# Pivot rows by transfers in the attention, and a router gate with stationary weights, in a fused transformer kernel

## The chip, the cores and the metric

The kernel runs on one core of a Trainium2 chip. The metric is the device time of one execution, in microseconds (us). TensorE multiplies matrices, VectorE, ScalarE and GpSimd work on tiles, and SyncE issues transfers. The profile calls them PE (PEld for the weight loads), DVE, ACT, POOL and SP.

## The reference, cut to what matters

Eight sequences (B) of 512 tokens (S) with 256 features (E) pass through four blocks: an attention with 16 heads, a mixture of 8 experts, a low-rank spectral product and a quaternion product. The change touches the expert gate and the orthogonalised mode matrix. Everything is float32.

```python
# gate of the experts
xn = rms_w * (x * jax.lax.rsqrt(var + EPS))
gate = xn @ wg_W + wg_b + (genre_embed @ gg_W + gg_b)
gate_w = jax.nn.softmax(gate, axis=-1)
topk_w, topk_i = jax.lax.top_k(gate_w, TOP_K)
...
# mode matrix, 64 x 64
gram = raw.T @ raw
chol = cholesky(gram + 0.0001 * eye, lower=True)
inv_chol = solve_triangular(chol, eye, lower=True)
q = raw @ inv_chol.T
signs = jnp.sign(jnp.sum(q * raw, axis=0, keepdims=True))
```

## The kernel before

**One order for all engines.** Pure Python functions write a list of steps, `order`. Each engine runs through this list in a program of its own and does its part of each step, so the place of a step in the list is its place in every queue. Semaphores carry the dependences. SyncE's program issues the transfers of a step when it comes to it, and waits first for what makes the data.

**Attention** (`attention_order`). There are 32 groups `i`, four to a sequence, of four heads each. A group is cut into 16 places, (k, n) with k and n from 0 to 3, and a place holds one `row` and one `col` step. A `row` step is a product of scores on TensorE (L1155, three PSUM banks in turn) and the maximum of each row on VectorE (L1628), which frees the bank: the product waits for the maximum three before it. A `col` step is the transposed product (L1170, with the mask's product L1174 or a seed by ScalarE L1360) and the exponential on ScalarE (L1355), over two banks. Every second k, a `weigh` pair multiplies the exponentials by the values (L1189): four heads on four groups of 32 columns of TensorE, 17 columns used. The maxima are split in two bf16 parts (`split_maxima`, L1638, L1640), turned on TensorE (`maxima_rows`) and sent by SyncE into the operands of the `col` steps (L967). Between them lie the projections of the next sequence (`project`), whose three bf16 parts are made by ScalarE, VectorE (`rest`) and GpSimd (`part`) and stored by SyncE (L925). At the end of every second k there is a piece of the experts' weights: SyncE stores chunk n-2 (L983), GpSimd splits chunk n-1 (L1864, L1866), SyncE fetches chunk n (L978).

**The chain of a sequence** (`chain`). After its attention each sequence passes its residual, its gate and its routing, one small step to a place. The residual's rows are turned (`turn_x1`, L1216) and copied to `x1T` by ScalarE (L1386), then come four `square_x1` on ScalarE, `root_x1` on GpSimd, four places later the `gate`, one place later `logits`. The gate takes the turned tokens as weights and moves the eight columns of `wg`: 4 tiles of tokens by 2 halves of the features, each float32 product being two instructions (L1227), and one product for the conditioning (L1229). Chains 0 to 5 lie in the attention, 6 and 7 in the experts.

**Experts** (`expert_order`). 39 tiles of 256 routed rows pass three layers (L1084) after their rows are turned (L1247). In a tile four places take a piece of `matrices`, once the chains are over.

**The mode matrix** (`matrices`). `gram` is one product on TensorE; `elim` holds the Gram matrix beside the transposed modes, 64 x 128. Each of the 63 `eliminate` steps spreads pivot row j over the partitions by a TensorE product with a broadcast column of the identity (L1099, two instructions), and VectorE (recorded under the helper's line L845) takes the reciprocal of the pivot, the factors, and the row update. TensorE waits for VectorE's step j-1, VectorE for TensorE's step j. Then come the norms, the quaternions and the combined matrices. Small products on TensorE take banks 6 and 7 in turn (`misc_bank`), and each waits till the one two before it is evicted.

## Time and profile before

| what | us |
|---|---|
| median of three runs | 1160.48 |
| lowest and highest | 1159.94, 1166.9 |
| the profiled execution | 1163.8 |
| its span, first to last instruction | 1162.1 |

The profile is one execution. Its granted TensorE clock is 0.996 of full speed. Busy times are those of an engine's own instructions. The ends of matmuls are modelled, so that neighbours overlap in the record; the distance of their starts is the safer measure. The attention's last row products start at 584 us; the first expert products start at 614 us; the mode matrix's steps lie from 785 to 988 us.

### The profile page before, as it was taken

What the parts mean: (1) busy time and instruction counts of PE and PEld (TensorE: products, weight loads), DVE (VectorE), ACT (ScalarE), POOL (GpSimd) and SP (SyncE); (2) the same over time, 40 slices, a digit from 0 to 9 for tenths busy, and PEclk for the clock granted to TensorE, in tenths of its full rate; (3) what the DMA queues carried; (4) which work ended last, traced back from release to release, by engine and by line L of the source; (5) the groups of instructions that cost most, each with busy time, mean ns of one, the idle gap of its engine ahead of it and who ended that gap; (6) DMA issues with size and microseconds to landing.
All of it is one profiled execution on the core that took longest, in us unless ns stands there. A gap on an engine that the chain in (4) does not pass through costs nothing.

```text
span 1162.1 us, 23399 instructions
## 1 busy us (share of the span) xinstructions
PE 1122.4 (97%) x7520; PEld 763.4 (66%) x7520; DVE 770.8 (66%) x2265; ACT 803.1 (69%) x1752; POOL 512.6 (44%) x837
## 2 busy tenths in 40 slices
PE   8899999999999999998989999999999999999988
PEld 4333434434334343342418999998999999999968
DVE  4877777787887878878745434355555555667747
ACT  2578888787787877877786756655666666666645
POOL 8424135583755837657462365354222223222220
PEclk8999999999999999999999999999999999999999
DMA  8665638367384572843837488856566766723536
GB/s 220 193 195 189 219 100 250 124 215 231 119 257 138 198 235 94 242 157 133 286 101 269 115 309 306 267 120 133 155 193 190 213 193 179 226 48 70 164 91 217
DMA packets 101616, 213.64 MB, mean 184 GB/s; under 512 B 10917, under 2 KB 71341, under 8 KB 93046
## 3 DMA queue, kind: packets, MB, share of 16 engines
q1 hardware_dynamic: 86038, 192.42, 51.1%
q0 software_dynamic: 14304, 18.69, 9.0%
q10 hardware_dynamic: 1152, 1.05, 0.4%
q8 instruction: 59, 0.97, 0.3%
q14 instruction: 63, 0.52, 0.1%
HBM read 239.28 MB, written 74.29 MB: 270 GB/s over the span
## 4 chain that ended last, share of the span: by engine, by line
PE 46%; ACT 3%; issue 1%; DVE 1%; POOL 1%; DMA 1%; another core or an unknown queue 0%; ACTq 0%; POOLq 0%
PE bank L1084 38%; PE bank L1247 1%; PE bank L1189 1%; PE bank L1099 1%; ACT pt L1355 1%; PE bank L1170 1%; DMA x<-yout,rows 1%; PE bank L1113 1%; PE bank L1174 1%; PE bank L1207 1%; PE bank L1282 0%; PE bank L1155 0%; PE bank L1227 0%; ACT full L1433 0%
## 5 line engine op out<-in xcount | busy, mean ns | idle before, releaser
L1628 DVE CUSTOM_DVE_ANT_0 junk<-bank,mneg 128x512 bf16<-128x512 f32 x512 | 333.0, 683 | 119.0 <-PE bank L1155 116.3
L1355 ACT ACTIVATE pt<-bank 128x512 f32<-128x512 f32 x512 | 301.0, 594 | 67.8 <-PE bank L1170 29.7
L1975 POOL DMA_INDIRECT x<-yout,rows x78 | 122.8, 1574 | 292.9 <-ACT yout L1438 249.6
L1084 PE MATMUL bank<-hid,w 128*128 128x256 f32 x1872 | 242.7, 286 | 4.2 <-DVE hid L1776 3.8
L1084 PEld LDWEIGHTS bank<-hid,w 128*128 128x128 f32 x1872 | 229.3, 190 | 6.0 <-issue 4.8
L1776 DVE TENSOR_TENSOR hid<-full,hid 128x256 fp32r<-128x256 f32 x312 | 133.3, 431 | 135.3 <-ACT full L1433 126.8
L1428 ACT ACTIVATE hid<-bank,biases 128x256 fp32r<-128x256 f32 x312 | 149.4, 479 | 91.6 <-PE bank L1084 88.0
L1433 ACT ACTIVATE full<-bank,biases 128x256 f32<-128x256 f32 x312 | 148.7, 477 | 0.0
L1174 PE MATMUL bank<-mneg,identb 128*128 128x512 bf16 x386 | 146.9, 381 | 0.0
L1084 PE MATMUL bank<-rowsT,w 128*128 128x256 f32 x936 | 122.9, 284 | 0.9 <-issue 0.9
L1084 PE MATMUL bank<-w,hid 128*128 128x256 f32 x936 | 121.9, 283 | 1.5 <-DVE hid L1776 1.5
L1189 PE MATMUL bank<-pt,vaug 128*17 128x512 f32 x1024 | 123.1, 598 | 0.0
L1084 PEld LDWEIGHTS bank<-rowsT,w 128*128 128x128 f32 x936 | 116.0, 190 | 1.7 <-issue 1.6
L1084 PEld LDWEIGHTS bank<-w,hid 128*128 128x128 f32 x936 | 115.1, 190 | 1.7 <-issue 1.7
L1438 ACT ACTIVATE yout<-yout,rows 128x256 f32<-128x256 f32 x78 | 39.3, 508 | 96.5 <-DVE yout L1782 96.5
L1170 PE MATMUL bank<-qst,kst 98*128 98x512 bf16 x256 | 97.5, 383 | 8.1 <-ACT pt L1355 6.3
L1155 PE MATMUL bank<-stacks 96*128 96x512 bf16 x256 | 97.6, 386 | 5.6 <-DVE rowmax L1628 4.4
L1155 PE MATMUL bank<-kst,qst 96*128 96x512 bf16 x256 | 97.8, 382 | 5.4 <-DVE rowmax L1628 4.8
L1170 PE MATMUL bank<-stacks 98*128 98x512 bf16 x256 | 97.5, 381 | 1.7 <-ACT pt L1355 1.0
L1866 POOL TENSOR_TENSOR w_parts<-w_parts 128x512 fp32r<-128x512 f32 x64 | 82.2, 1285 | 5.2
L1360 ACT ACTIVATE bank<-mneg 128x512 f32<-128x512 bf16 x124 | 74.6, 602 | 4.0
L1965 POOL DMA_INDIRECT routed<-xw,idx x64 | 64.1, 1001 | 17.1 <-issue 13.5
(184 smaller groups left out, 1445.2 us busy)
## 6 DMA issues: line engine op xcount, KB each, us to landing
w<-split_weights SPq DMA_DIRECT2D x80, 1024.0 KB
w<-split_weights SPq DMA_DIRECT2D x40, 2048.0 KB
split_weights<-w_parts SPq DMA_DIRECT2D x64, 512.0 KB, 3.8
w_parts<-in_W SPq DMA_DIRECT2D x64, 256.0 KB, 4.3
split_parts<-parts SPq DMA_DIRECT2D x28, 384.0 KB, 2.6
rows<-routed SPq DMA_DIRECT2D x39, 258.0 KB, 3.4
stacks<-split_parts SPq DMA_DIRECT2D x36, 256.0 KB, 5.2
qst<-split_parts SPq DMA_DIRECT2D x24, 256.0 KB, 5.3
```

The lines of the kernel that those rows point to most:

```text
L1084: product = T.matmul(ps, w[p], x[q], start=(k == 0 and n == 0), stop=(k == len(weights) - 1 and n == 2))
L1155: T.matmul(bank[n % 3][:, :], qst[b % 2][0:KQ, h, st * P:(st + 1) * P], kst[b % 2][0:KQ, h, :], start=True, stop=True).then_inc(row_scored ...
L1170: product = T.matmul(ps[:, :], kst[b % 2][0:KQ + SHIFTS, h, kt * P:(kt + 1) * P], qst[b % 2][0:KQ + SHIFTS, h, :], start=not seed, stop=li ...
L1174: product = T.matmul(ps[:, :], identb[:, :], mneg[:, 1, kt, :], start=False, stop=True)
L1189: product = T.matmul(bank[5][32 * hh:32 * hh + D + 1, :], vaug[b % 2][:, kt, h, :], pt[col_place[gi, kt, hh] % len(pt)][:, :], start=(kt = ...
L1355: A.activation(pt[n % len(pt)][:, :], bank[3 + n % 2][:, :], ACT.Exp, scale=float(D) ** -0.5).then_inc(exped.sem, 1)
L1428: A.activation((hid1, hid2)[n - 1][j % 2][0][:, m, :], ps[:, 0:TW], ACT.Relu, bias=biases[j % NS][:, column:column + 1])
L1433: A.activation(full[place % len(full)][:, :], ps[:, 0:TW], ACT.Relu, bias=biases[j % NS][:, column:column + 1]).then_inc(rectified.sem, 1)
L1628: V.tensor_tensor_reduce(junk[n % 2][:, :], bank[n % 3][:, :], mneg[:, 0, st, :], 1.0, FLOOR, ALU.add, ALU.max, rowmax[gi % 2][:, hh, st:s ...
L1776: V.tensor_tensor(lo, h[:, :], hi.bitcast(F32), ALU.subtract).then_inc(hidden_low.sem, 1)
L1866: G.tensor_tensor(w_parts[n][:, 1], w_parts[n][:, 1].bitcast(F32), w_parts[n][:, 0].bitcast(F32), ALU.subtract).then_inc(w_low.sem, 1)
L1975: G.indirect_dma_start(x2_dram, bass.IndirectOffsetOnAxis(ap=rows[j % NS][:, tt, E + 1:E + 2].bitcast(U32), axis=0), yout[j % NY][:, tt], ...
```

## The change

- The gate's weights (`wg`, widened with zeros to 32 columns) become the stationary operand, on four column groups, one for each tile of 128 tokens; the tokens (`x1T`) move, 128 columns each. The result has the experts on partitions. ScalarE copies it into `x1T`'s first 128 columns (`gate_rows`), TensorE turns it with one transpose (`turn_gate`), and ScalarE copies the logits (`copy_logits`). `gate`, `gate_rows` and `turn_gate` now lie behind the second, third and fourth `square_x1`, `copy_logits` one place after `root_x1`, and `logits` stays at its place.
- The conditioning's part of the logits is computed once for all sequences (`cond_gate`), from a product `condX` made in `prepare`.
- The pivot row is no longer spread by TensorE. SyncE sends row j of `elim` to 64 partitions of `pivot_row[j % 2]` (`send_pivot`), and VectorE reads it from there. `gram` moves into group 2 of the attention, and 58 eliminations into groups 3 to 31, two a group, at place n = 2 of k = 0 and k = 2, each with the sending of the next pivot at n = 3. Five stay in the experts, with three pieces' pause ahead of each.
- `m2` is stored without gaps, with fewer zeros to set.

```diff
     for st in range(ST):
         out.append(("square_x1", b, st))
         yield
+        if st:
+            out.append((("gate", b), ("gate_rows", b), ("turn_gate", b))[st - 1])
     out.append(("root_x1", b))
+    yield
+    out.append(("copy_logits", b))
     for _ in range(4):
         yield
-    out.append(("gate", b))
-    yield
     out.append(("logits", b))
...
 def matrices(out):
 
-    out.append(("gram",))
-    yield
-    for j in range(KB - 1):
+    for j in range(ATTENTION_PIVOTS, KB - 1):
+        for _ in range(3):
+            yield
         out.append(("eliminate", j))
-        yield
+        if j + 1 < KB - 1:
+            out.append(("send_pivot", j + 1))
...
+                if n == 2 and k % 2 == 0 and PIVOT_GROUP <= i < GROUPS:
+                    j = 2 * (i - PIVOT_GROUP) + k // 2
+                    if j < ATTENTION_PIVOTS:
+                        out.append(("eliminate", j))
+                        pivots.append(("send_pivot", j + 1))
+                if (n, k) == (3, 2) and i == PIVOT_GROUP - 1:
+                    out.append(("gram",))
+                    pivots.append(("send_pivot", 0))
+                elif n == 3 and pivots:
+                    out.append(pivots.pop(0))
...
+            elif name == "send_pivot":
+                j, = at
+                sp.wait_ge(*matrix.at(("eliminate", j - 1) if j else ("gram",)))
+                start(pivot_row[j % 2][:, :], elim[j:j + 1, :].unsqueeze(1).to_broadcast([1, KB, 2 * KB])).then_inc(dma_pivot[j % 2], 16)
...
-            elif name == "eliminate":
-                j, = at
-                ps = take(misc_bank(step))
-                pe.wait_ge(ident_made, 2)
-                pe.wait_ge(*matrix.at(("eliminate", j - 1) if j else ("gram",)))
-                pe.wait_ge(constants_made, CONSTANTS)
-                T.matmul(ps[:, 0:2 * KB], ident[:, j:j + 1].to_broadcast([P, P]), elim[:, :],
-                         start=True, stop=True).then_inc(side_pe.sem, 1)
...
-                for st in range(ST):
-                    for k in range(KT):
-                        T.matmul(ps[:, st * NX:(st + 1) * NX], x1T[:, k, st * P:(st + 1) * P], wg[:, k],
-                                 start=(k == 0), stop=(k == KT - 1))
-                T.matmul(ps[:, ST * NX:(ST + 1) * NX], condR[:, b:b + 1].to_broadcast([C + 2, P]), ggw[:, :],
-                         start=True, stop=True).then_inc(gated.sem, 1)
+                for k in range(KT):
+                    for st in range(ST):
+                        product = T.matmul(ps[GW * st:GW * (st + 1), 0:P], wg[:, k], x1T[:, k, st * P:(st + 1) * P],
+                                           start=(k == 0), stop=(k == KT - 1))
+                product.then_inc(gated.sem, 1)
+            elif name == "turn_gate":
+                b, = at
+                ps = take(misc_bank(step))
+                pe.wait_ge(*gate_rows.at((b,)))
+                pe.wait_ge(ident_made, 2)
+                T.transpose(ps[:, 0:P], x1T[:, 0, 0:P], ident[:, :]).then_inc(gate_turned.sem, 1)
...
-                ps, _ = misc_bank(step)
+                row = pivot_row[j % 2]
                 dve.wait_ge(constants_made, CONSTANTS)
-                dve.wait_ge(*side_pe.at(step))
-                v(V.reciprocal, pivot[:, 0:1], ps[0:KB, j:j + 1])
+                dve.wait_ge(dma_pivot[j % 2], 16 * (j // 2 + 1))
+                v(V.reciprocal, pivot[:, 0:1], row[:, j:j + 1])
                 v(V.scalar_tensor_tensor, pivot[:, 1:2], elim[0:KB, j:j + 1], pivot[:, 0:1], below[:, j:j + 1], ALU.mult, ALU.mult)
-                v(V.scalar_tensor_tensor, elim[0:KB, :], ps[0:KB, 0:2 * KB], pivot[:, 1:2], elim[0:KB, :], ALU.mult, ALU.add)
+                v(V.scalar_tensor_tensor, elim[:, :], row[:, :], pivot[:, 1:2], elim[:, :], ALU.mult, ALU.add)
```

## Rows read from the trace of the kernel before

**Rows 1.** Busy time by stretch: PE, PEld, DVE, ACT, POOL, clock, DMA, GB/s.

```profile
250.00:300.00 50.00, 49.92 (x288) 22.60 (x281) 38.57 (x116) 39.31 (x81) 26.09 (x65) 1.00 0.68 205
...
1000.00:1050.00 50.00, 50.00 (x422) 50.00 (x421) 32.76 (x106) 32.38 (x80) 12.44 (x8) 1.00 0.40 83
```

**Rows 2.** TensorE groups by form: count, busy us, mean ns, idle us before.

```profile
L1099 PE MATMUL bank<-elim,ident 128*128 128x128 f32 x126 | 24.2, 273 | 2.4 <-DVE elim L845 1.4 <-issue 0.9
```

**Rows 3.** Timeline of TensorE, experts: start us, us, line, operation, count.

```profile
856.42 0.60 PE L1247 MATMUL bank<-ident,rows 128*128 128x128 f32 x4
...
869.17 0.60 PE L1247 MATMUL bank<-ident,rows 128*128 128x128 f32 x4
...
1008.16 0.60 PE L1247 MATMUL bank<-ident,rows 128*128 128x128 f32 x4
...
1020.05 0.60 PE L1247 MATMUL bank<-ident,rows 128*128 128x128 f32 x4
```

**Rows 4.** Timeline of TensorE at the fourth elimination step; idle time in brackets.

```profile
797.40 0.46 PE L1099 MATMUL bank<-elim,ident 128*128 128x128 f32 x2 [1.44 <-DVE elim L845]
```

**Rows 5.** Timeline of TensorE at a weighing and a gate in the attention.

```profile
200.50 1.91 PE L1189 MATMUL bank<-pt,vaug 128*17 128x512 f32 x16
...
202.34 0.39 PE L1155 MATMUL bank<-stacks 96*128 96x512 bf16 x1
...
202.79 1.85 PE L1227 MATMUL bank<-wg,x1T 128*128 128x8 f32 x16
...
204.72 1.11 PE L1207 MATMUL bank<-wo,oT_last 128*128 128x256 f32 x4
```

**Rows 6.** Timeline of ScalarE and TensorE where the gate's transposition would stand.

```profile
271.32 0.42 ACT L1303 ACTIVATE squared<-xw 128x256 bf16<-128x256 f32 x1
...
271.92 0.38 PE L1155 MATMUL bank<-kst,qst 96*128 96x512 bf16 x1
```

**Rows 7.** VectorE's groups by form, and below them two rows of its timeline.

```profile
L845 DVE RECIPROCAL pivot<-bank 64x1 f32<-64x1 f32 x63 | 9.6, 152 | 0.0
...
L845 DVE SCALAR_TENSOR_TENSOR pivot<-elim,pivot,below 64x1 f32<-64x1 f32 x63 | 13.3, 211 | 2.2
...
L845 DVE SCALAR_TENSOR_TENSOR elim<-bank,pivot,elim 64x128 f32<-64x128 f32 x63 | 21.6, 343 | 2.2
...
L1640 DVE TENSOR_TENSOR m<-rowmax,m 128x16 bf16<-128x16 f32 x32 | 11.6, 362 | 1.1
...
L1472 DVE TENSOR_TENSOR gt<-flts,gs 128x32 f32<-128x32 f32 x16 | 8.2, 516 | 0.6
...
239.49 1.12 DVE L1638 CAST m<-rowmax 128x16 bf16<-128x16 f32 x1
...
240.64 0.23 DVE L1640 TENSOR_TENSOR m<-rowmax,m 128x16 bf16<-128x16 f32 x1
```

**Rows 8.** Waits between 60 and 590 us: total us, times, longest.

```profile
DVE junk L1628 <- PE bank L1155: 109.4, 97, 2.6
```

**Rows 9.** Timeline of VectorE behind the first and the last place of a step.

```profile
61.67 0.08 DVE L1628 DVE_READ_ACCUMULATOR2_ANT rowmax<- 128x1 f32 x1
...
63.40 0.69 DVE L1628 CUSTOM_DVE_ANT_0 junk<-bank,mneg 128x512 bf16<-128x512 f32 x1 [1.65 <-PE bank L1155]
...
580.37 0.08 DVE L1628 DVE_READ_ACCUMULATOR2_ANT rowmax<- 128x1 f32 x1
```

**Rows 10.** Waits of SyncE, its transfers, its timeline, and a row of VectorE's.

```profile
SPq L925 <- POOL parts L1833: 165.8, 28, 14.6
...
split_parts<-parts SPq DMA_DIRECT2D x28, 384.0 KB, 2.6
...
240.56 0.38 SPq L925 DMA_DIRECT2D split_parts<-parts  x1
...
240.98 0.49 SPq L983 DMA_DIRECT2D split_weights<-w_parts  x1
...
242.58 0.08 DVE L1628 DVE_READ_ACCUMULATOR2_ANT rowmax<- 128x1 f32 x1
```

More of the change, by code:

```diff
@@ L53 @@
 TOPK = 2
+GW = P // ST
 NTILES = B * S * TOPK // TW + NX - 1
@@ L259, in finish_steps @@
         return [("project_o", b, st) for st in range(ST)] + [("chain", b)]
-    chains, todo, rests, parted = [], [], [], []
+    chains, todo, rests, parted, pivots = [], [], [], [], []
     def work_off():
@@ L501, in _build @@
     below = lasting("below", [KB, KB])
-    elim = lasting("elim", [P, 2 * KB])
+    elim = lasting("elim", [KB, 2 * KB])
+    pivot_row = [lasting(f"pivot_row{i}", [KB, 2 * KB]) for i in range(2)]
     raw = lasting("raw", [KB, 2, KB])
@@ L565, in _build @@
     rowmax = [sb(f"rowmax{i}", [P, GH, ST]) for i in range(2)]
-    m2 = [sb(f"m2_{i}", [P, ST, P], BF16) for i in range(2)]
+    m2 = [sb(f"m2_{i}", [P, (ST - 1) * GH * SHIFTS + P], BF16) for i in range(2)]
     mrow = [sb(f"mrow{i}", [GH * SHIFTS, S], BF16) for i in range(2)]
@@ L637, in _build @@
     gated = signal("gated", of("gate"))
+    gate_turned = signal("gate_turned", of("turn_gate"))
+    cond_gated = signal("cond_gated", of("cond_gate"))
     counted = signal("counted", of("place"))
-    side_pe = Signal(sem("side_products"), [s for s in order if s[0] in ("gram", "eliminate", "mixed", "combined")])
+    side_pe = Signal(sem("side_products"), [s for s in order if s[0] in ("gram", "mixed", "combined")])
     rows_turned = signal("rows_turned", of("turn"))
@@ L653, in _build @@
     x1T_ready = signal("x1T_ready", of("turn_x1"))
-    logits_ready = signal("logits_ready", of("gate"))
+    gate_rows = signal("gate_rows", of("gate_rows"))
+    logits_ready = signal("logits_ready", of("copy_logits"))
+    cond_ready = signal("cond_ready", of("cond_gate"))
     gate_exped = signal("gate_exped", of("gate_exp"))
@@ L735, in _build @@
     dma_quat = sem("dma_quat")
+    dma_pivot = [sem(f"dma_pivot{i}") for i in range(2)]
     dma_x2 = [sem(f"dma_x2_{i}") for i in range(NL)]
     dma_out = [sem(f"dma_out{i}") for i in range(2)]
-    CONSTANTS = 23
+    CONSTANTS = -1 + 25
     MASKS = 4
@@ L1198, in tensor_program @@
                 for st in range(ST):
-                    product = T.matmul(ps[:, st * P:(st + 1) * P], m2[gi % 2][:, st], identb[:, :], start=True, stop=True)
+                    product = T.matmul(ps[:, st * P:(st + 1) * P], m2[gi % 2][:, st * GH * SHIFTS:st * GH * SHIFTS + P], identb[:, :], start=True, stop=True)
                 product.then_inc(max_turned.sem, 1)
@@ L1632, in vector_program @@
                 found = rowmax[gi % 2][:, :, :]
-                first_part, second_part = (m2[gi % 2][:, :, k * GH:(k + 1) * GH].rearrange("p s h -> p h s") for k in range(SHIFTS))
+                first_part, second_part = (m2[gi % 2][:, 0:ST * GH * SHIFTS].rearrange("p (s k h) -> p k h s", s=ST, k=SHIFTS)[:, k] for k in range(SHIFTS))
                 dve.wait_ge(constants_made, CONSTANTS)
```

60 lines of the change are left out of this document (42 added, 18 removed).

## The prediction

> **What bounds the kernel now.** I read the busy shares by stretch first. In the attention (a stretch around 275 us) and in the experts (1000 to 1050 us) TensorE is busy 49.9 and 50.0 us of 50; VectorE stands at 38.6 and 32.8 [rows 1]. TensorE is the bound in both stages, so what counts is what its queue is relieved of, and what new makes it stand still. Next I read TensorE's own record of the experts, for the pitch of a tile; then its record of a gate; then VectorE's groups and waits in the attention, and last the queue of SyncE, which has to send the pivot rows.
>
> **Experts: 63 matmul pairs leave TensorE.** A group by form gives 24.2 us busy for 126 instructions [rows 2], but that is not their price, because they overlap their neighbours. The tile's pitch is: with four elimination steps in it, it takes from 856.42 to 869.17, 12.75 us; with none, from 1008.16 to 1020.05, 11.89 us [rows 3]. That is 0.215 us a step, and 63 x 0.215 = 13.5 us. Ahead of one pair TensorE stood 1.44 us for VectorE's earlier step [rows 4]; the product behind it waited for nothing else, so 1.4 us more go. Together -14.9; the bounds are -13.5 (the wait is inherited by the next product) and -25.6 (the busy time). The five steps left there use no TensorE; each has three pieces' time to its pivot, some 9 us, and I cost them at nothing. Without that cover each would hold VectorE, and with it the low halves that TensorE's next layer needs.
>
> **Gate: 8 times.** Now it lasts from 204.72 back to 202.79, 1.93 us, with the conditioning pair inside [rows 5]. After: 16 instructions on four column groups, 128 columns each. The kernel has the same pattern in the weighing, 16 instructions with 512 columns in 200.50 to 202.34, 1.84 us [rows 5]. If time goes with columns, the gate takes 0.46; if it goes with instructions, 1.84. I take 0.8: nearer the first, as the columns are a quarter, and above it, as the weight loads do not shrink. The transposition added costs 0.60 / 4 = 0.15, by the transposes of the experts' rows [rows 3]. So 0.95 against 1.93, 8 x -0.98 = -7.8, and +0.3 once for the conditioning product: -7.5, between -10.3 and +0.8. The transposition waits for ScalarE's copy of the gate's rows. ScalarE would reach that place at 271.32 and need some 0.25 us; TensorE would reach its own at 271.92 [rows 6]. So the wait is mostly hidden; for the one batch where it isn't I add 0.5.
>
> The Trainium skill (TensorEngine Tiling (Array Packing), Tiling Modes) says that tiles work independently and can load and multiply in parallel. That speaks for the 0.46; the weighing at 1.84 us for 16 agrees with it as far as it goes.
>
> **Attention: 58 steps join VectorE.** A step is 0.152 + 0.211 + 0.343 us [rows 7], with gaps 0.75. VectorE idles 109.4 us for rows' products between 60 and 590 us [rows 8], and 58 x 0.75 = 44 fits in the sum; but not at every place. A row product waits for the maximum three before it. I laid a delay at each of the 58 places into VectorE's record (the first after the maximum that ends at 61.75, with 1.65 us idle behind it, the last after the one that ends at 580.45), let it run down in the idle times that follow, and counted what went beyond the start of the product three later [rows 9]. That is work on recorded times, not a measurement. It gives 4.4 us at 0.75 us a step, 8.5 at 1.05, 18 at 1.5, 32 at 1.95, 42 at 2.25: steep, since idle time is used up.
>
> What does a step really cost? First, VectorE's operations that read two operands from SBUF are longer here than their shortest: the second part of the maxima has a mean of 362 ns where a single one took 230, a comparison has 516 in the mean, and the cast that leads the maxima's split once took 1.12 us [rows 7]. The pivot row now comes from SBUF, so two of the three operations are of that kind. I add 0.15 each: 1.05 us a step.
>
> The Trainium skill (SBUF — State Buffer, Who interferes with whom) gives the cause: a VectorE instruction with two SBUF inputs locks against a GpSimd instruction that reads SBUF, and one with a single SBUF input does not. By that rule the old step, whose row came from PSUM, was exempt in its last operation and the new one is not. The trace's 362 and 516 agree.
>
> Second, transfers can be late. A pivot is sent one place after the step that makes it and used eight places later, about 9 us. SyncE sends in order, and it stands 165.8 us in all, up to 14.6, before the parts of the projections [rows 10]. The tightest place, in the middle of a batch: SyncE is done with such a part at 240.94 (the chunk's store follows at 240.98), and VectorE's row maxima reach the next step at 242.66 [rows 10]. A part of 384 KB lands 2.6 us after its issue [rows 10]; a pivot behind it lands at about 243.7. So it is about 1 us late. Holding SyncE's record against VectorE's at all 58 places gives such room of 1.7 us at eight (two each in the batches from group 12 to 25), and 4.3 us or more at the others. Eight steps with 1 us more raise the loss from 8.5 to 15.4; with 0.3 to 9.9. Some of what TensorE stands there ScalarE uses to catch up, and I take 13. The ends are 4.4 (no wait, no lock) and 42.
>
> The Trainium skill (DMA: Bandwidth & Descriptors, Queues, rings and completion order) states that the semaphore write of a transfer lands only after earlier writes of that DMA engine. It speaks against the change: a small pivot can't overtake a large part. No row before shows it alone.
>
> SyncE's own 58 issues, about 0.4 us each, lie in its idle time. SyncE now also waits for VectorE at each place; behind it stand the store and fetch of a weight chunk, which have half a group's time to the next. ScalarE gets eight copies of about 0.25 us and loses nothing that counts. I cost these at nothing; if that cover goes, GpSimd's chunk work is late, and after it the parts.
>
> **Sum.** -14.9 - 7.5 + 0.5 + 13 = -8.9 us against the profiled execution of 1163.8 us (span 1162.1), so 1154.9. That execution lies 3.3 us above the median of 1160.5; against the median it is **1151.6 us**.
>
> **Rivals.**
> - *All covered*: no late pivot and no lock, attention loss 4.4. Then -17.5: 1143.0. For it speaks the idle sum; against it the eight tight places. 0.18.
> - *VectorE becomes the bound* (slower): pivots late not at eight places but at most, since SyncE waits for GpSimd, GpSimd for VectorE, and both now slip. At 2.25 us a step the loss is 42, the sum +20: 1180.6. It decides from about 1.75 us a step (loss 22, no gain), and is over 1% slower from 2.0. Against it: 4.3 us of room or more at 50 places. 0.18.
> - *The lock at full strength*: GpSimd is busy 26.1 of 50 us [rows 1]; if each of the two operations meets it half of the time and waits 0.7 us then, a step costs 1.5, and with late pivots the loss is about 25: +3, so 1163.6 against the median. 0.09. The rule is that of the Trainium skill's page SBUF — State Buffer, told above.
> - *The change relieves less*: gate in 1.84 us, the wait inherited: -13.5 + 0.8 + 0.5 + 13 = +0.8, 1161.3. 0.10.
> - *The forecast*: 0.45, by its own terms 1144 to 1158.
>
> **How the numbers follow.** About 1%, 11.6 us, is what a measurement can tell from no change. 1% faster is below 1148.9: all covered, 0.17, and half of the forecast, 0.22; 0.39. Within 1%: the other half, 0.23, and the two cases around 1162, 0.18; 0.41. Slower, over 1172.1: 0.18 and tails, 0.20. The range that leaves 2 in 10 out goes from 1141 to 1173, the slow end into the VectorE case.
>
> **What would show it.** A tile in the experts at 11.9 us throughout from 800 us on. A gate in about 0.8 us. In the attention, idle time of TensorE for VectorE's maxima up by some 10 us, at groups 13, 17, 21 and 25 above all, and VectorE waiting for the pivot's landing at those eight places alone. Two-operand steps with a mean over 230 ns and single ones over 1 us. I am wrong if VectorE waits for pivots all along, if the attention doesn't lengthen, or if the tile still takes 12.7 us.

## The result, and the profile after

| kernel | median us | lowest to highest | span of the profiled execution |
|---|---|---|---|
| before, beside it (four runs) | 1160.31 | 1159.94 to 1166.9 | 1162.1 |
| changed | 1178.28 | 1176.15 to 1180.99 | 1174.4 |

The ratio is 1.0127, with a 95% interval of 1.0096 to 1.0159: slower by 14.7 us. The quotient of the two medians in the table is 1.0155, or 18.0 us, at the far end of that interval; below, the ratio is used. The forecast of 1151.6 was on the wrong side, and its range ended at 1173.

Two places tell where the time went, in the two profiled executions. The last row maximum of the attention ends at 589.7 us before and at 616.1 after, 26.4 later; the end of the span comes only 12.3 later. So the attention lost 26, and the experts gained 14.

First the parts that went as forecast. Busy times by stretch, as in [rows 1], then the timeline of TensorE at four tiles of the experts, as in [rows 3], and the gate in the timeline of TensorE with the groups of its two operations, as in [rows 5]:

```profile
250.00:300.00 50.00, 44.94 (x254) 18.90 (x257) 40.31 (x128) 37.54 (x83) 24.85 (x57) 0.97 0.76 221
1000.00:1050.00 50.00, 50.00 (x425) 50.00 (x424) 20.84 (x47) 32.99 (x80) 14.81 (x10) 1.00 0.59 178
...
855.68 0.60 PE L1279 MATMUL bank<-ident,rows 128*128 128x128 f32 x4
867.43 0.60 PE L1279 MATMUL bank<-ident,rows 128*128 128x128 f32 x4
...
1011.52 0.60 PE L1279 MATMUL bank<-ident,rows 128*128 128x128 f32 x4
1023.43 0.60 PE L1279 MATMUL bank<-ident,rows 128*128 128x128 f32 x4
...
202.98 0.64 PE L1248 MATMUL bank<-x1T,wg 128*32 128x128 f32 x16
203.56 0.39 PE L1176 MATMUL bank<-stacks 96*128 96x512 bf16 x1
...
205.33 0.30 PE L1256 MATMUL bank<-ident,x1T 128*128 128x128 f32 x1 [0.29 <-ACT x1T L1431]
205.47 1.03 PE L1160 MATMUL bank<-wv,xT 128*128 128x256 f32 x4
...
L1248 PE MATMUL bank<-x1T,wg 128*32 128x128 f32 x128 | 5.2, 279 | 0.7
L1256 PE MATMUL bank<-ident,x1T 128*128 128x128 f32 x8 | 2.4, 303 | 2.0 <-ACT x1T L1431 1.8
```

The tile at 855 us took 12.75 before and takes 11.75 now, and the later one still 11.9. A gate is 0.64 us in the record and its transposition 0.30, but the rows behind them start 0.58 and 0.14 later, and the price before (1.93) was such a distance of starts. What is wrong stands in the first line: in the attention TensorE is busy 44.9 of 50 us where it was 49.9.

Then the elimination's groups on VectorE in the attention (60 to 600 us), and its waits there, as in [rows 7, 8]; the second pair of lines is from 60 to 616 us. The 58th step lies behind 600 us, so the groups have 57:

```profile
L870 DVE SCALAR_TENSOR_TENSOR elim<-pivot_row,pivot,elim 64x128 f32<-64x128 f32 x57 | 26.2, 459 | 2.0
L870 DVE SCALAR_TENSOR_TENSOR pivot<-elim,pivot,below 64x1 f32<-64x1 f32 x57 | 18.9, 332 | 2.0
L870 DVE RECIPROCAL pivot<-pivot_row 64x1 f32<-64x1 f32 x57 | 8.6, 151 | 15.9 <-DMA pivot_row<-elim 15.9
...
DVE junk L1671 <- PE bank L1176: 66.2, 80, 1.5
DVE pivot L870 <- DMA pivot_row<-elim: 15.9, 10, 2.7
```

A step is 0.151 + 0.332 + 0.459 us, with gaps some 1.0, as forecast (1.05). VectorE used up 43 of its 109 us of idle time. And it stood 15.9 us for pivot rows, ten times.

Last, one of the four longest of these waits, in the order in which it builds up: SyncE's queue, VectorE, GpSimd beside it, TensorE.

```profile
247.38 0.38 SPq L950 DMA_DIRECT2D split_parts<-parts  x1
247.81 0.49 SPq L1013 DMA_DIRECT2D pivot_row<-elim  x1
...
249.40 0.08 DVE L1671 DVE_READ_ACCUMULATOR2_ANT rowmax<- 128x1 f32 x1
252.05 0.15 DVE L870 RECIPROCAL pivot<-pivot_row 64x1 f32<-64x1 f32 x1 [2.57 <-DMA pivot_row<-elim]
252.24 0.64 DVE L870 SCALAR_TENSOR_TENSOR pivot<-elim,pivot,below 64x1 f32<-64x1 f32 x1
252.92 1.21 DVE L870 SCALAR_TENSOR_TENSOR elim<-pivot_row,pivot,elim 64x128 f32<-64x128 f32 x1
...
251.72 2.26 POOL L1876 TENSOR_TENSOR parts<-rest,parts 128x512 bf16<-128x512 f32 x2
...
249.75 0.38 PE L1191 MATMUL bank<-stacks 98*128 98x512 bf16 x1
249.97 0.38 PE L1176 MATMUL bank<-kst,qst 96*128 96x512 bf16 x1
...
250.61 0.38 PE L1195 MATMUL bank<-mneg,identb 128*128 128x512 bf16 x1
254.79 0.61 PE L1176 MATMUL bank<-kst,qst 96*128 96x512 bf16 x1 [3.80 <-DVE rowmax L1671]
255.19 0.63 PE L1191 MATMUL bank<-stacks 98*128 98x512 bf16 x1
255.62 0.63 PE L1195 MATMUL bank<-mneg,identb 128*128 128x512 bf16 x1
```

SyncE stands for the part until 247.38 and sends the row behind it. The row lands 4.2 us after its issue. VectorE waits 2.57 us, then both two-operand operations are long (0.64 and 1.21 where the shortest are 0.21 and 0.34) beside two operations of GpSimd that fill 251.72 to 253.98, and TensorE stands 3.80 us. Read the starts of TensorE's rows after that: they come every 0.43 us, where the same products came every 0.22 before the stall. TensorE now runs at 1.2 GHz, the lower of its two levels. The same pattern comes at groups 13, 17, 21 and 25. The stretches that follow, with the granted clock in the last column but two:

```profile
254.80:258.20 3.40, 3.40 (x12) 1.47 (x13) 3.37 (x11) 1.62 (x5) 1.88 (x2) 0.50 0.79 238
333.30:336.70 3.40, 3.18 (x12) 1.48 (x12) 3.37 (x10) 2.72 (x8) 1.45 (x2) 0.50 0.90 257
411.80:415.20 3.40, 3.18 (x12) 1.46 (x12) 3.37 (x10) 3.01 (x10) 1.04 (x2) 0.50 0.77 211
486.90:493.70 6.80, 4.45 (x14) 1.93 (x15) 6.38 (x17) 2.64 (x8) 3.20 (x4) 0.50 0.89 281
```

Added up over the whole span, the stretches at 1.2 GHz are 12 us before and 48 us after.

### The profile page after: what moved, and what is told of

Read it like the earlier page. It is cut to its first block, busy times and chain, and to the rows that moved or that the text cites. A ratio compares the mean times of both kernels' runs of the same rounds, so it can differ in the third digit from the quotient of the medians.

```text
span 1174.4 us, 23150 instructions
## 1 busy us (share of the span) xinstructions
PE 1107.8 (94%) x7335; PEld 742.6 (63%) x7388; DVE 777.4 (66%) x2266; ACT 805.4 (69%) x1761; POOL 511.7 (44%) x838
## 3 DMA queue, kind: packets, MB, share of 16 engines
q10 hardware_dynamic: 1152, 1.05, 0.4%
## 4 chain that ended last, share of the span: by engine, by line
PE 41%; DMA 3%; POOL 2%; ACT 1%; issue 1%; DVE 1%; SPq 1%; POOLq 0%; DVEq 0%; ACTq 0%
PE bank L1113 36%; DMA x<-yout,rows 2%; PE bank L1279 1%; PE bank L1228 1%; PE bank L1134 1%; DMA out<-fin 1%; POOL routed L2010 1%; PE bank L1210 1%; PE bank L1176 0%; DMA routed<-xw,idx 0%; POOL x L2020 0%; PE bank L1191 0%; DMA w_parts<-in_W 0%; POOL gt L870 0%; POOL run L870 0%
## 5 line engine op out<-in xcount | busy, mean ns | idle before, releaser
L1113 PE MATMUL bank<-hid,w 128*128 128x256 f32 x1872 | 237.4, 286 | 7.0 <-DVE hid L1819 7.0
L1469 ACT ACTIVATE hid<-bank,biases 128x256 fp32r<-128x256 f32 x312 | 151.9, 487 | 84.8 <-PE bank L1113 84.5
L1474 ACT ACTIVATE full<-bank,biases 128x256 f32<-128x256 f32 x312 | 151.6, 486 | 0.0
L1195 PE MATMUL bank<-mneg,identb 128*128 128x512 bf16 x333 | 129.6, 389 | 0.0
L1113 PE MATMUL bank<-w,hid 128*128 128x256 f32 x936 | 118.6, 282 | 1.5 <-DVE hid L1819 1.5
L1113 PE MATMUL bank<-rowsT,w 128*128 128x256 f32 x936 | 118.1, 282 | 1.7 <-ACT full L1474 0.9
L1176 PE MATMUL bank<-stacks 96*128 96x512 bf16 x256 | 100.5, 398 | 18.0 <-DVE rowmax L1671 15.3
L1908 POOL CAST w_parts<-w_parts 128x512 fp32r<-128x512 f32 x64 | 39.9, 624 | 113.5 <-DMA w_parts<-in_W 113.5
```

What stands on the lines that cost most here:

```text
L1113: product = T.matmul(ps, w[p], x[q], start=(k == 0 and n == 0), stop=(k == len(weights) - 1 and n == 2))
L1176: T.matmul(bank[n % 3][:, :], qst[b % 2][0:KQ, h, st * P:(st + 1) * P], kst[b % 2][0:KQ, h, :], start=True, stop=True).then_inc(row_scored ...
L1195: product = T.matmul(ps[:, :], identb[:, :], mneg[:, 1, kt, :], start=False, stop=True)
L1469: A.activation((hid1, hid2)[n - 1][j % 2][0][:, m, :], ps[:, 0:TW], ACT.Relu, bias=biases[j % NS][:, column:column + 1])
L1474: A.activation(full[place % len(full)][:, :], ps[:, 0:TW], ACT.Relu, bias=biases[j % NS][:, column:column + 1]).then_inc(rectified.sem, 1)
```

## The experiments

Every ratio is against the kernel before on the same chip, with its 95% interval; "us" behind a ratio is its distance from 1, times 1160.3. The intervals are 2 to 6 us either way, so two runs less than some 5 us apart are not told apart. Times of single places, such as the end of the last maximum, are each from one profiled execution.

### 1. The two halves alone

The kernel before, with the gate's part of the change only (its products, `gate_rows`, `turn_gate`, `copy_logits`, `cond_gate`, the gapless `m2`):

> The kernel before with the gate's part of the change alone: weights stationary, the transposition, the conditioning once for all. The pivots stay TensorE products in the experts. My theory (the gate is not at fault; in the changed kernel its eight products take 0.65 us each and the transpositions 0.3, against 1.93 before) expects -7 to -8 us, so about 1153. The rival that the gate at its new place makes TensorE wait expects 1160 or more, with waits of TensorE at the transposition.

Measured: 0.9913 (0.9891 to 0.9935), -10.1 us. The forecast had -7.0 for it, just outside the interval (-7.5).

The changed kernel with the gate as before, so only the pivot rows move:

> The pivots' part of the change alone, the gate as before. If the gate helps by 7 to 8 us also beside the pivots, this is slower than the whole change: about 1186. If the gate is what hurts, it is below 1178.

Measured: 1.0163 (1.0144 to 1.0181), +18.9 us; eleven waits for rows in the whole execution, up to 2.7 us. The whole loss belongs to the pivot rows. The two halves add up to +8.8, the whole change has +14.7; the rest of 6 us is beyond the intervals only narrowly, and I have no cause for it.

### 2. The row ahead of the part

```diff
                         out.append(("eliminate", j))
-                        pivots.append(("send_pivot", j + 1))
+                        out.append(("send_pivot", j + 1))
```

The row is sent right behind its step and no longer behind the part.

> The whole change, with the sending of the pivot row right behind its elimination in SyncE's queue, ahead of the store of a projection's part, for which SyncE waits. In the changed kernel VectorE waits 2.5 to 2.7 us for the pivot row in groups 13, 17, 21 and 25, TensorE then stands up to 3.8 us, and the granted clock falls to half behind each of these places. Theory A (late rows and the clock behind them) expects these four waits and the four spells of half clock to be gone: 4 x 2.5 us of waits and about 8 us of clock, so about 1162, with the waits of 0.7 to 1.1 us in groups 11, 15, 19, 23 still there. Theory B (VectorE's added work of 58 us alone is too much) expects 1172 or more.

Measured: 0.9983 (0.9963 to 1.0002), -2.0 us: 16.7 us better than the change. The waits at groups 13, 17, 21 and 25 fell from 2.5-2.7 us to 0.2-0.7, and TensorE's four stalls from 3.5-3.8 to under 1 us. No stretch at 1.2 GHz is left there. In the four late batches that is 11 us of stalls, and the rest is what comes with them. The total of the waits for rows fell only to 11.9 us, since others grew (3.65 us at group 3; 1.6, 1.2 and 2.0 at k = 0 of groups 11, 19 and 23). The profiled execution took 1167.3 us, 5.6 above the median of its ten, and its last maximum ends at 609.4; so the traces show less of the gain than the times do.

### 3. The clock by itself

The late rows stay, and TensorE gets twelve products of no use ahead of each stall:

```diff
+                if i in (13, 17, 21, 25) and (k, n) == (1, 1):
+                    out.append(("filler", i))
...
+            elif name == "filler":
+                ps = take(misc_bank(step))
+                pe.wait_ge(masks_made, MASKS)
+                for _ in range(12):
+                    product = T.matmul(ps[:, :], identb[:, :], mneg[:, 1, 0, :], start=True, stop=True)
```

> The whole change, with twelve more products of 128x512 bf16 (2.6 us at full clock, results unused) in TensorE's queue in groups 13, 17, 21 and 25, ahead of the product that stands there for up to 3.8 us. The late rows stay. If the half clock follows from TensorE standing still (theory A), the four spells at these places are gone or fewer, the products themselves are covered by the wait, and the time falls by 4 to 8 us, to about 1172. If the clock falls for another reason, or if the products cost more than they cover, the time is 1178 or more and the spells are at their places.

Measured: 1.0082 (1.0055 to 1.0109), +9.5 us. The timeline of TensorE at the same stall, and two of the stretches quoted above:

```profile
250.47 2.75 PE L1258 MATMUL bank<-mneg,identb 128*128 128x512 bf16 x12
254.38 0.39 PE L1179 MATMUL bank<-kst,qst 96*128 96x512 bf16 x1 [1.16 <-DVE rowmax L1680]
254.61 0.38 PE L1194 MATMUL bank<-stacks 98*128 98x512 bf16 x1
...
254.80:258.20 3.40, 3.07 (x17) 1.17 (x16) 3.37 (x12) 2.96 (x9) 1.74 (x2) 1.00 0.81 248
...
486.90:493.70 6.80, 6.47 (x40) 2.02 (x38) 6.34 (x21) 5.72 (x15) 3.95 (x13) 1.00 0.62 186
```

VectorE's rows are as late as before (2.56, 2.57, 2.96 and 2.65 us), and the product behind the stall starts 4.13 us after the last one ahead of it, where it took 4.18. But the clock stays at 2.4 GHz and the starts 0.22 us apart, at all four places. The ratios differ by 5.2 us, with intervals that overlap. The traces say much the same: TensorE's stall where the maxima of the last groups run out ends at 566.7 us and not at 571.8, though the last maximum ends only 3.5 us earlier (612.6), behind a late row at group 31 (1.7 us) that the change does not have. So with 48 products more the attention is some 4 to 5 us shorter, and I take 5 as the clock's price; it is the least certain of the terms. Over the whole span 20 us less are spent at the lower level, 17 of them in the four stretches quoted above, and that gave back 5 and not 10. In three of the four stretches VectorE is busy 3.3 of 3.4 us or more at either clock, so it sets much of the pace itself.

### 4. VectorE's load, SyncE's stops, the transfers

In four versions VectorE reads constant rows and waits for none, so the mode matrix is not computed. They differ in what SyncE does. First nothing:

```diff
-                sp.wait_ge(*matrix.at(("eliminate", j - 1) if j else ("gram",)))
-                start(pivot_row[j % 2][:, :], elim[j:j + 1, :].unsqueeze(1).to_broadcast([1, KB, 2 * KB])).then_inc(dma_pivot[j % 2], 16)
...
-                dve.wait_ge(dma_pivot[j % 2], 16 * (j // 2 + 1))
```

> The whole change without any pivot transfer: VectorE reads constant rows from SBUF, so the mode matrix isn't computed, while VectorE's three operations a step, their places and operands' forms stay. What is left of the loss in the attention is that of VectorE's work and its lock against GpSimd. Theory A expects no wait for rows at all and fewer spells of half clock: about 1158. Theory B expects 1172 or more, and TensorE's waits for row maxima as in the changed kernel.

Then the stop alone: the same kernel, with only the `sp.wait_ge(*matrix.at(...))` of the first removed line put back.

> Constant pivot rows on VectorE and no transfer, as in the run without transfers (1145.6 us), but SyncE still stops at each of the 63 places until VectorE's elimination step before it is done, as in the run with unused transfers (1156.8 us). The mode matrix isn't computed here. If SyncE's stops alone cost (its chunk loads go out later, GpSimd's splits start later and fall beside VectorE's elimination), the time is 1154 to 1159 us, GpSimd's waits for chunks come to about 110 us and the elimination's operations are about 13 us over their minimum. If the transfers themselves cost (queue, memory), the time is 1143 to 1149 us, with GpSimd's waits near 67 us and 6.5 us over the minimum.

Then the stop and a transfer of a constant row, which VectorE doesn't wait for (SyncE itself waits here for its transfer two before, by then some 15 us old):

```diff
+                start(pivot_row[j % 2][:, :], const_row[j:j + 1, :].unsqueeze(1).to_broadcast([1, KB, 2 * KB])).then_inc(dma_pivot[j % 2], 16)
```

> The whole change with all 63 transfers issued at their places, behind the same waits of SyncE, but of a constant row, and VectorE reads constants without waiting for them; the mode matrix isn't computed. It holds what transfers do to others (SyncE's queue, GpSimd's chunks, the memory), without VectorE's waits. If only the waits and the clock behind them cost (theory A), about 1146 to 1149, as without transfers. If the transfers and SyncE's waits cost by themselves, 1153 or more, with GpSimd's wait for chunks near the 113 us of the changed kernel.

And the same with 512 bytes a transfer in place of 32 KB:

```diff
-                start(pivot_row[j % 2][:, :], const_row[j:j + 1, :].unsqueeze(1).to_broadcast([1, KB, 2 * KB])).then_inc(dma_pivot[j % 2], 16)
+                start(pivot_row[j % 2][0:1, :], const_row[j:j + 1, :]).then_inc(dma_pivot[j % 2], 16)
```

> The run with unused transfers (ratio 0.9954), but each of the 63 transfers moves one row of 512 bytes to one partition, not 32 KB to 64 partitions. The mode matrix isn't computed here. The run with SyncE's stops alone had 0.9892, so 0.6% (7 us) hang on the transfers. If the traffic of the 64 copies costs, the ratio is 0.988 to 0.991 and the elimination's operations are 8 to 9 us over their minimum, as without transfers. If it is the issue on SyncE's queue and what it shifts, the ratio stays at 0.994 to 0.997 and the excess at 13 to 14 us.

"Elimination's excess" is the time that the two VectorE operations with two SBUF operands took above 211 and 343 ns, their means in the kernel before [rows 7], summed over the 58 steps of the attention, in us. "Long" counts those of the 116 operations that took over 1.3 times as much.

| SyncE does | ratio, interval | us | last maximum ends | GpSimd waits for chunks | elimination's excess | long |
|---|---|---|---|---|---|---|
| nothing | 0.9854 (0.9817 to 0.9892) | -16.9 | 588.8 | 53.9 | 6.8 | 14 |
| stop | 0.9892 (0.9861 to 0.9924) | -12.5 | 594.7 | 78.1 | 8.9 | 16 |
| stop, 512 bytes | 0.9904 (0.9873 to 0.9935) | -11.1 | 596.0 | 85.2 | 8.6 | 16 |
| stop, 32 KB | 0.9954 (0.9931 to 0.9976) | -5.3 | 602.0 | 97.9 | 14.3 | 26 |
| the change: stop, 32 KB, awaited | 1.0127 (1.0096 to 1.0159) | +14.7 | 616.1 | 99.6 | 13.5 | 27 |

The fifth column is this view (waits of GpSimd between 60 and 600 us), for the first and the fourth:

```profile
POOL w_parts L1907 <- DMA w_parts<-in_W: 53.9, 17, 12.5
...
POOL w_parts L1914 <- DMA w_parts<-in_W: 97.9, 30, 9.6
```

The load on VectorE costs little: with the gate's part alone the last maximum ends at 585.3, with 58 steps on VectorE besides at 588.8, 3.5 us later (the ratios leave 8). The first run had been expected at 1158 at best and came to 1145.6. From there to the unused transfers is 11.6 us, with intervals that lie apart. Neither of my two theories of it alone is right: SyncE's stops move chunk loads (the waits of GpSimd grow with each line of the table), and the 32 KB carry more weight than the issue, since the short transfers cost hardly more than the stop. The stop alone came to 1151.6 us, between the ranges of both theories; the short transfers landed in the range of "the traffic costs" (0.988 to 0.991). Between neighbouring lines of these four the intervals overlap, so the split of the 11.6 is a leaning; the sum is shown. The last line lies apart from them: waiting for the rows costs 20.0 us more.

The last two columns show what lengthens the elimination. Each long operation, in every line, runs while GpSimd runs one of its own, and of the operations that met no GpSimd instruction none, in any line, is over its mean by more than 4 ns. Their excess is about half a microsecond apiece in every line, so it is their number that grows. Of the long ones 8 stand beside GpSimd's chunk work (`w_parts`) without SyncE's stops, and 21 with stops and 32 KB: the late chunks fall upon the steps. (In the change it is 12, and most of the others stand beside the projections' parts.) That the meeting is the cause is read from the overlap in time; no run here takes GpSimd's work away.

### 5. Fewer steps, where a batch is tight

```diff
-ATTENTION_PIVOTS = min(KB - 1, 2 * (GROUPS - PIVOT_GROUP))
+PIVOT_PLACES = [(i, k) for i in range(PIVOT_GROUP, GROUPS) for k in (0, 2) if (i % NG, k) not in ((2, 0), (3, 0))]
+ATTENTION_PIVOTS = min(KB - 1, len(PIVOT_PLACES))
```

The row goes right behind its step, from SyncE. 43 steps lie in the attention and 20 in the experts.

> The whole change, sent first as in the earlier run, and without elimination steps at k = 0 of the third and fourth group of each sequence (VectorE has the four scalings there, and the row was late there by 0.7 to 3.7 us): 43 steps in the attention, 20 in the experts with three pieces' pause. Theory A expects no wait for rows over 1 us in the attention and little more of TensorE's waits for maxima than without transfers: 1146 to 1150. If SyncE's and the transfers' mere presence is what costs, it stays near the 1161.7 of the kernel that only sends first.

Measured: 0.9892 (0.9844 to 0.9940), -12.5 us. Waits for rows are down to 2.0 us in five. It beats both kernels, but not clearly the gate alone (0.9913). The median, 1148.7, is within what was expected.

### 6. The chunk work moved by one k: a miss

```diff
-            n, step = divmod((i - 1) * ST + k, 2)
+            n, step = divmod((i - 1) * ST + k + 1, 2)
```

Since the loss seemed to be a meeting of chunk work and elimination, I moved the one away from the other, with 43 steps and with 58 (row right behind its step in both).

> The version with 43 steps in the attention and the row sent ahead of the part (1148.7 us), with the chunk work (store, split, fetch of SyncE and GpSimd) moved one step on, behind the parts of odd k instead of even k. If it is the meeting of the chunk work with the elimination step on SyncE's queue and on the shared port that costs, the time falls to 1144 to 1148 us; if the place of the chunk work is of no weight, it stays at 1148 to 1150 us; over 1151 us the shift makes GpSimd's splits late.

> The version with 58 steps and the row sent ahead of the part (1161.7 us), with the same shift of the chunk work by one step. By the theory that the chunk work collides with the elimination steps, 1153 to 1158 us and fewer us over the minimum in the elimination than 10.8; by the theory that only the late rows and the clock set the rest, 1160 to 1163 us.

Measured: 0.9986 (0.9970 to 1.0001) in place of 0.9892, and 1.0053 (1.0013 to 1.0094) in place of 0.9983: slower by 11 and by 8 us. With 43 steps no row is late in the attention, and yet TensorE runs at 1.2 GHz for 6.8 us in each of four batches. VectorE's timeline there,

```profile
247.46 0.69 DVE L1634 TENSOR_TENSOR rest<-bank,parts 128x512 f32<-128x512 f32 x1 [3.06 <-POOL parts L1876]
...
249.47 1.50 DVE L870 SCALAR_TENSOR_TENSOR pivot<-elim,pivot,below 64x1 f32<-64x1 f32 x1
```

and GpSimd's timeline ahead of it:

```profile
240.09 0.60 POOL L1908 CAST w_parts<-w_parts 128x512 fp32r<-128x512 f32 x1
...
246.16 1.17 POOL L1876 TENSOR_TENSOR parts<-rest,parts 128x512 bf16<-128x512 f32 x1
```

The chunk's split now stands ahead of a projection's part in GpSimd's queue (without the shift it comes behind it), the part is late, and VectorE stands for it: 11.8 us in four, a wait that neither the kernel before nor the version without the shift has. The elimination's operations did not get shorter either (an excess of 11.2 us, 3.0 without the shift). With 58 steps the time lies above both ranges expected; with 43 it is the third outcome that was named (over 1151 us), but it is a projection's part that is late and not a split. The old phase was the good one, and my theory of how to cure the meeting was wrong.

### 7. The rows from ScalarE's queue

```diff
-                sp.wait_ge(*matrix.at(("eliminate", j - 1) if j else ("gram",)))
-                start(pivot_row[j % 2][:, :], elim[j:j + 1, :].unsqueeze(1).to_broadcast([1, KB, 2 * KB])).then_inc(dma_pivot[j % 2], 16)
...
+                act.wait_ge(*matrix.at(("eliminate", j - 1) if j else ("gram",)))
+                nc.scalar.dma_start(pivot_row[j % 2][:, :], elim[j:j + 1, :].unsqueeze(1).to_broadcast([1, KB, 2 * KB])).then_inc(dma_pivot[j % 2], 16)
```

58 steps, the order of the change (a row one place behind its step):

> The changed kernel (ratio 1.0127) with the 63 pivot rows sent from ScalarE's queue, at their old places, one place behind each step, in place of SyncE's. If SyncE's order and stops are what costs (a row behind a part, chunk loads and splits late), the waits for rows fall under 5 us, GpSimd's waits for chunks return to about 67 us and the ratio falls to 0.985 to 0.992. If the traffic or VectorE's load costs, the ratio stays over 1.0. The rival for this run: ScalarE itself stands at each place until VectorE's step is done, its exponentials are late, and TensorE's waits for ScalarE's pt go over 15 us: ratio 0.995 or more.

Measured: 0.9951 (0.9933 to 0.9969), -5.7 us: 20 us better than the change, for its queue alone. One row is late (2.8 us), and GpSimd waits 58.1 us for chunks. ScalarE stands 15.6 us in ten for `elim`. The ratio stayed a little above what the theory had (0.985 to 0.992) and is that of the rival (0.995 or more), but TensorE's products stand only 6.5 us for ScalarE's `pt`, where the rival asked for over 15.

43 steps, the row right behind its step:

> The version with 43 steps in the attention, each row sent right behind its step (ratio 0.9892), with the rows sent from ScalarE's queue in place of SyncE's. By the theory that SyncE's stops cost the rest, the ratio falls to 0.980 to 0.987, the fastest of all; if ScalarE's own standing costs as much, 0.988 to 0.993; if ScalarE's exponentials become the bound, over 1.0.

Measured: 0.9990 (0.9966 to 1.0014), -1.2 us, against 0.9892 from SyncE's queue, and between the ranges expected. The timeline of ScalarE and of TensorE at group 13:

```profile
246.56 0.47 ACTq L1426 DMA_DIRECT2D pivot_row<-elim  x1
247.08 0.63 ACT L1354 ACTIVATE parts<-rest 128x512 bf16<-128x512 f32 x1 [2.69 <-DVE elim L870]
...
248.25 0.61 PE L1187 MATMUL bank<-stacks 98*128 98x512 bf16 x1 [2.36 <-ACT pt L1383]
248.65 0.63 PE L1191 MATMUL bank<-mneg,identb 128*128 128x512 bf16 x1
249.07 0.63 PE L1172 MATMUL bank<-kst,qst 96*128 96x512 bf16 x1
```

ScalarE stands 2.69 us until VectorE's step is done, TensorE 2.36 us for the exponential behind it, and then the starts are 0.42 us apart. It is the stall of the change again, with another engine in it. So the next three move the sending away from the step: 43 steps and one place, 43 steps and three places, 58 steps and three places.

```diff
-                elif n == 3 and pivots:
+                elif n == 1 and pivots:
                     out.append(pivots.pop(0))
```

(That is the edit for three places; `send_pivot` is put on `pivots` again, as in the change, and in the experts it comes a piece after its step.)

> The version with 43 steps in the attention whose rows go from ScalarE's queue, but each row is sent one place behind its step, not right behind it (then: ratio 0.999, ScalarE stood for VectorE's elimination, the longest time 2.8 us, and TensorE then for ScalarE's pt, 13.2 us). If ScalarE's standing was what cost, its waits for elim fall under 5 us and the ratio falls to 0.983 to 0.990. If the 43 steps on ScalarE's queue cost in another way, it stays above 0.994.

> The same with the row sent three places behind its step in the attention and a piece later in the experts. ScalarE's waits for elim should be near zero; a row then still has five places, some 5.5 us, against the 3.5 to 3.8 us to landing. By the theory that the stop of the sending engine costs, 0.981 to 0.988 and not slower than the version with one place. If late rows take over (waits for pivot_row over 5 us), 0.99 or more.

> 58 steps in the attention, rows from ScalarE's queue three places behind each step (one place: ratio 0.9951, ScalarE's waits for elim some 14 us). By the theory that the stop of the sending engine costs, 0.986 to 0.992. If VectorE's load of 58 steps is the rest, it stays at 0.993 to 0.997, and the version with 43 steps lies below it.

| steps in the attention, row sent | ratio, interval | median us | last maximum ends | ScalarE waits for `elim` | waits for rows, 60 to 616 us |
|---|---|---|---|---|---|
| 43, right behind | 0.9990 (0.9966 to 1.0014) | 1165.5 | 602.3 | 17.4 (and 4.2 for `pivot`) | 0 |
| 43, one place | 0.9882 (0.9849 to 0.9916) | 1147.9 | 589.7 | 6.9 | 0 |
| 43, three places | 0.9822 (0.9791 to 0.9852) | 1141.8 | 587.8 | none | 0 |
| 58, one place | 0.9951 (0.9933 to 0.9969) | 1160.5 | 601.8 | 15.6 | 2.8 |
| 58, three places | 0.9960 (0.9935 to 0.9986) | 1159.9 | 603.5 | none | 17.3 |

The medians in this table come from two chips; compare the ratios. From "right behind" to "one place" the gain is clear of noise, from one to three places the intervals touch. With one place ScalarE still stood 6.9 us, more than the 5 that were expected.

With 43 steps and three places ScalarE stands for no step and VectorE for no row in the attention. This is the fastest version, and the only one whose interval lies under that of the gate alone (0.9891 to 0.9935): 20.7 us below before by the ratio (the medians on that chip are 1141.8 and 1163.8). The last maximum ends 1.9 us earlier than in the kernel before, with 43 steps laid into VectorE. TensorE's waits from 60 to 600 us, in which the change has 25.4 us for maxima:

```profile
PE bank L1174 <- DVE rowmax L1673: 7.0, 13, 1.4
PE bank L1189 <- ACT pt L1385: 4.4, 13, 0.5
```

The run with 58 steps came out in its expected range, but not by the reason I gave, VectorE's load. Its rows are late: eight waits up to 4.2 us, six of them at k = 0 of groups 7, 15, 19, 23, 27 and 31. The longest, in ScalarE's queue and VectorE's timeline, with the transfers between 350 and 362 us:

```profile
351.10 0.47 ACTq L1427 DMA_DIRECT2D pivot_row<-elim  x1
...
361.26 0.16 DVE L871 RECIPROCAL pivot<-pivot_row 64x1 f32<-64x1 f32 x1 [4.18 <-DMA pivot_row<-elim]
...
qst<-split_parts SPq DMA_DIRECT2D x2, 256.0 KB, 8.9
...
xT<-in_xT SPq DMA_DIRECT2D x1, 512.0 KB, 9.4
pivot_row<-elim ACTq DMA_DIRECT2D x1, 32.0 KB, 10.1
```

The 32 KB need 10.1 us, on a queue of their own, at a batch's end, where the next sequence's operands are loaded and the DMA engines are busy nine tenths of these 12 us. What of the two makes the row late is not shown. The version with 43 steps has no step at the k = 0 of groups 11, 15, 19 and so on, and so doesn't meet them.

## Why the prediction was wrong, point by point

- **Experts, -14.9: right.** The tile is 11.75 to 11.9 us from 820 us on, but for one of 14.0 at 962; the one from 804.5, with the clock at 0.50 for 3.4 us in it, took 15.55. From the last maximum to the end it is 572.4 us before and 558.3 after, -14.1, with two of the eight gates in it and 10 us at 1.2 GHz against it.
- **Gate, -7.5 and +0.5: right in mechanism, a little low.** By the distance of starts a gate costs 0.58 us where I had 0.8 (nearer still to the 0.46 by columns), and its transposition 0.14 where I had 0.15. TensorE's waits for ScalarE's copy are 1.8 us in all eight, where I had 0.5. With these prices the sum would have been -7.6 in place of -7.0, and the part alone gave -10.1 (-12.6 to -7.5), so up to 2.5 us of it stay unexplained.
- **A step of 1.05 us: right.** 1.01 in the attention and 0.78 in the experts. The two-operand operations have means of 332 and 459 ns, where the kernel before had 211 and 343 [rows 7], and single ones are 1.2 to 1.5 us. The row's move from PSUM to SBUF does not cost by itself: the five steps left in the experts read SBUF too and take 211 and 344 ns. The long ones all run beside a GpSimd instruction (27 of 27 in the change). The rule of the Trainium skill (SBUF — State Buffer, Who interferes with whom) that the prediction weighed agrees with that; the trace shows the company and not the lock.
- **Its cost when all is on time, 8.5: right in order.** 3.5 us by the ends of the last maximum, 8 by the ratios (-16.9 against -10.1 with -14.9 in the experts). Laying delays into the record gave the right order here; on one case, and with a factor of two between the two measures, that may be luck in part.
- **Late rows: right places, wrong size.** I named groups 13, 17, 21 and 25, and there the longest waits are. But the delay was 1.0 us in my sum and 2.5 to 2.7 in the run, since I gave a row behind a part 2.6 to 2.7 us to its landing, the part's own time [rows 10], and it needs 4.2. The room itself was right: from the row's issue to VectorE's arrival I had 1.7 us, and it is 1.67 (247.81 to 249.48). Of the eight places four were late, and six others that I had given 4.3 us of room: a row behind the loads of a batch's end (sent at 281.12, awaited until 287.94, in the lines below) needs 6.8. This step failed: a landing time read off one other transfer was taken as a constant, and the late rows were priced at 4.5 us (13 less 8.5). In its place stand 3.8 us to the landing in the median and up to 9.0 in the change, and a price of 20.0 us for awaiting the rows, the clock's 5 in it.

```profile
281.12 0.54 SPq L1013 DMA_DIRECT2D pivot_row<-elim  x1
...
287.94 0.15 DVE L870 RECIPROCAL pivot<-pivot_row 64x1 f32<-64x1 f32 x1 [0.70 <-DMA pivot_row<-elim]
```

- **SyncE's stops and 58 transfers at nothing: wrong, 11.6 us.** This is the second step that failed. The prediction named the cover ("half a group's time to the next") and what would be late without it: GpSimd's chunk work. It was. GpSimd's waits for chunks rose from 54.5 to 99.6 us. I had argued from SyncE's idle time, but that idle time is waits in order, and a stop among them moves all behind it.
- **The clock: not in the prediction at all.** 5 us for four stretches by the filler run. The rows quoted there showed a granted clock of 1.00 [rows 1], and I took it for a given. At the four late batches it fell behind a stall of 3.5 to 3.8 us. The granted clock of the kernel before was not always full either: it was 0.50 from 547.7 to 551.1 us, behind a stall of 1.27.
- **The sum.** The attention's term was 13. By the ends of the last maximum, against the gate alone (585.3), it is 30.8: VectorE's load 3.5, SyncE's stops and transfers 13.2, the rows awaited 14.1, with the clock in it. These are differences of single profiled executions; the ratios give 11.6 and 20.0 for the last two. The run with the row ahead of the part fits them: it lies 3.3 us above the one with unused transfers, with 11.9 us of waits for rows left.
- **The rivals.** The time fell beside that of "VectorE becomes the bound" (1180.6), but not by its mechanism at the strength it asked for: rows were late at ten places and not at most, and a step with its wait is 1.01 + 15.9 / 58 = 1.3 us, under the 1.75 where that case began. The closeness to its number is luck. Its reason, the slip through SyncE and GpSimd, is half of the truth; I had used it only to make rows late, and it costs by itself. The size of "all covered" (-17.5) was reached only by another program, the one with 43 steps from ScalarE's queue (-20.7).
- **The Trainium skill's rule on the order of landings** (DMA: Bandwidth & Descriptors, Queues, rings and completion order) spoke against the change, and I gave it 1 us at eight places. With the row ahead of the part 16.7 us came back, which agrees with it. The row on ScalarE's own queue needed 10.1 us too in company of large loads. That does not speak against the rule, which that page states for each DMA engine, across its queues; but the engines were nine tenths busy then, and no run here parts their order from their load.

## What to carry to other kernels

A small transfer in a chain of steps costs twice: where it is awaited (20.0 us here) and where it is issued, even if nobody waits for it (11.6 us). So ask who stands at the issue and what lies behind it in that queue, and send it when the data is already there. Take a landing time from a transfer sent in the same company, and keep such chains away from the places where large loads go out. And where TensorE is the bound, price a stall of some microseconds above its own length, and look at the granted clock of the stretch behind it.

## What the runs showed of the hardware that I had not expected

- Behind stalls of 2.2 to 3.8 us TensorE's products of 512 columns came every 0.43 us in place of 0.22, for 3.4 to 6.8 us, at a granted clock of 0.50. Twelve useless products ahead of the same stalls kept it at 1.00; the ratios with and without them are 1.0082 and 1.0127, with intervals that overlap.
- A transfer of 32 KB from SBUF to SBUF landed in 3.8 us in the median of the change's 63 (the row below, from its list of transfers), 4.2 behind a part, 6.3 to 7.7 at the six other late rows, and 10.1 on another queue beside a batch's loads.

```profile
pivot_row<-elim SPq DMA_DIRECT2D x63, 32.0 KB, 3.8
```

- VectorE's update with two SBUF operands, 343 ns at its shortest, took up to 1452 ns, and the factors (64 x 1) up to 1186 in place of 211. All the long ones, in every run, stand beside a GpSimd instruction. Transfers of 32 KB that they don't depend on raised their number from 16 to 26 of 116, as GpSimd's late chunk work fell upon them.
